# A fused decoder of two layers: expert weights spread by DMA, and new orders of work in three phases

## The reference

```python
x = ln(x + self_attention(x))            # layer 0: 16 heads, window of 32
x = ln(x + cross_attention(ctx, x))      # layer 0: one head of 128
x = ln(x + experts(x))                   # layer 0: 8 experts of 512, gelu, 2 of 8 by softmax
x = ln(x + state_space(x))               # layer 1: returns x + out itself, so x counts twice
x = ln(x + cross_attention1(x, ctx))     # layer 1: 16 heads of 64, inner width 1024
x = ln(x + experts1(x))                  # layer 1: 8 experts of 256 and a shared one, silu gate
```

```python
combined = sum_e w[:, e] * down_e(h_e(x))    # w from the top 2 of the router's logits
```

## Time and profile before

| | |
|---|---|
| median of 3 runs | 2001.07 us (1999.9 to 2002.27) |
| profiled execution | 1998.59 us, of which 1996.9 us are the span from first to last instruction |
| granted TensorE clock, mean | 0.941 of full |
| busy in the span | PE 88%, DVE 80%, ACT 59%, POOL 42% |
| moved by DMA | 264.97 MB, 133 GB/s in the mean |

### The profile page before, as it was taken

How to read it: one execution, slowest core, us unless ns; L and a number is a source line. 1 busy time by engine, 2 the same in 40 slices (tenths; PEclk the granted TensorE clock), 3 DMA queues, 4 the chain that set the end, 5 groups by cost and what they waited for, 6 DMA issues and landing times. The chain is left out here.

```text
span 1996.9 us, 34496 instructions
## 1 busy us (share of the span) xinstructions
PE 1750.6 (88%) x10381; PEld 1266.5 (63%) x10381; DVE 1593.3 (80%) x2986; ACT 1186.7 (59%) x1868; POOL 830.3 (42%) x705
## 2 busy tenths in 40 slices
PE   4886888699956379999999999999999999994997
PEld 3554656688842256666667666766666676654886
DVE  3884676678867379988998999899889988966887
ACT  2441332577732167777777777777777777754553
POOL 4660111223342373636364545455454546322333
PEclk9997998699976589999999999999999999997998
DMA  5101775100000079898989888989888998971000
GB/s 192 77 0 62 301 279 233 43 1 0 1 0 0 32 157 206 174 192 178 193 175 192 184 189 178 186 186 182 188 179 191 179 196 173 190 127 72 6 5 10
DMA packets 623534, 264.97 MB, mean 133 GB/s; under 512 B 601565, under 2 KB 605693, under 8 KB 622717
## 3 DMA queue, kind: packets, MB, share of 16 engines
q1 hardware_dynamic: 623468, 264.19, 57.1%
HBM read 112.24 MB, written 0.92 MB: 57 GB/s over the span
## 5 line engine op out<-in xcount | busy, mean ns | idle before, releaser
L2234 DVE SCALAR_TENSOR_TENSOR xa_h<-xa_psum,xa_rinv,xa_h 128x500 f16<-128x500 f32 x672 | 452.5, 729 | 0.7 <-ACT xa_h L2349 0.7
L2333 ACT ACTIVATE xa_psum<-xa_psum,xa_negmax 128x1500 f32<-128x1500 f32 x224 | 332.7, 1485 | 198.0 <-DVE xa_negmax L2219 198.0
L2349 ACT ACTIVATE xa_h<-xa_psum,xa_rinv 128x1000 f16<-128x1000 f32 x448 | 372.2, 883 | 82.5 <-DVE xa_rinv L2226 81.2
L2215 DVE TENSOR_REDUCE xa_psum<-xa_psum 128x1 f32<-128x1000 f32 x224 | 269.5, 1203 | 88.1 <-PE xa_psum L2089 88.1
L2087 PE MATMUL xa_psum<-xa_c_hi,xa_q_hi 128*128 128x500 f32 x672 | 282.9, 421 | 28.5 <-DVE xa_h L2234 18.3
L2112 PE MATMUL xa_psum<-xa_prT,xa_n_hi 128*128 128x512 f16 (+1 forms) x768 | 272.9, 355 | 2.4 <-DMA xa_prT<-xa_h 1.5
L2114 PE MATMUL xa_psum<-xa_prT,xa_n_lo 128*128 128x512 f16 (+1 forms) x768 | 270.7, 352 | 0.0
L2113 PE MATMUL xa_psum<-xa_prT,xa_n_hi 128*128 128x512 f16 (+1 forms) x768 | 270.7, 352 | 0.0
L2088 PE MATMUL xa_psum<-xa_c_lo,xa_q_hi 128*128 128x500 f32 x672 | 262.5, 391 | 0.0
L2089 PE MATMUL xa_psum<-xa_c_hi,xa_q_lo 128*128 128x500 f32 x672 | 262.2, 390 | 0.0
L2219 DVE TENSOR_REDUCE xa_negmax<-xa_psum 128x1 f32<-128x512 f32 x224 | 154.9, 691 | 25.8
(11 more groups left out here) (303 smaller groups left out, 3613.8 us busy)
## 6 DMA issues: line engine op xcount, KB each, us to landing
ctxN<-in_ctxP SPq DMA_DIRECT2D x16, 1536.0 KB, 9.2
xa_ctxP<-in_ctxP SPq DMA_DIRECT2D x32, 768.0 KB, 4.4
ctxT<-in_ctxT SPq DMA_DIRECT2D x16, 1500.0 KB, 6.3
xa_ctxT<-in_ctxT SPq DMA_DIRECT2D x32, 750.0 KB, 4.9
xa_prT<-xa_h SPq DMA_TRANSPOSE x192, 5.5
up<-in_F_up SPq DMA_DIRECT2D x1, 2048.0 KB, 9.2
down<-in_F_down SPq DMA_DIRECT2D x1, 2048.0 KB, 13.3
gate<-in_F_gate SPq DMA_DIRECT2D x1, 1024.0 KB, 4.8
```

The source lines that it names most:

```text
L2215: nc.vector.tensor_reduce(psum[:, bank + 1, W:W + 1], psum[:, bank:bank + 2, 0:W], AX.XY, ALU.max)\
L2234: nc.vector.scalar_tensor_tensor(h[:, H_SLOT[s], 1, a:z], psum[:, bank + j, 0:W], rinv[:, s % 2, :], h[:, H_SLOT[s], 0, a:z], ALU.mult, AL ...
L2333: nc.scalar.activation(psum[:, bank:bank + 3, 0:W], psum[:, bank:bank + 3, 0:W], ACT.Exp, bias=negmax[:, s % 2, :], accum_out=rs[:, s % 2, ...
L2349: nc.scalar.activation(h[:, H_SLOT[s], 0, a * W:z * W].rearrange("p (a c) -> p a c", c=W), psum[:, bank + a:bank + z, 0:W], ACT.Identity, ...
```

## The change

Six edits.

1. **Spread weights (expert phases).** The transposes, the copies from PSUM and POOL's copy are gone. At the end of routing the weights of all pairs are transposed once on PE, copied once (ACT in layer 0, DVE in layer 1), and stored by 16 DMAs of SP to an array in DRAM, rows by expert; the routing phase waits for the stores. In the expert phase SP loads, for each chunk, two halves of four experts, broadcast to 128 partitions, 1 MB each.
2. **PSUM waits.** The tail's transposes share no bank with spread products any more.
3. **State space.** `bout` is added by PE: a product of a row of ones with the bias row starts the accumulation in PSUM, and DVE adds twice the residual in the same operation as before. POOL's two additions are gone. PE multiplies `chosen` ahead of the tail's transposes.
4. **Self attention.** The bias row is added to all of `x_tok` once, on DVE, ahead of the steps. DVE, PE, ACT and POOL get another order; `attend` is cut in two.
5. **First cross attention.** The logits move to a step of their own (lag 6). The values are cut in three, tops in two halves, and all engines' orders change.
6. The scratch area that the compiler keeps for dynamic DMAs is set to 2,048 bytes.

```diff
# experts: load of the spread weights, and their use
+            def load(i, half):
+                sp.wait_ge(part_ready, last(i, (half + 1) * EH, NE))
+                sp.sem_inc(issuing, 1)
+                sp.dma_start(spread[:, half * EH:(half + 1) * EH, :].rearrange("p e (g t) -> p e g t", g=CK),
+                             k.weight_rows[layer][half * EH:(half + 1) * EH, bass.ds(i * CK, CK), :].partition_broadcast(128))\
+                    .then_inc(spread_loaded[half], 16)
-                def spread_weights(e):
-                    for p in range(CK):
-                        done = nc.tensor.transpose(psum[:, 6 + e % 2, p * 128:(p + 1) * 128],
-                                                   wc[:, p, e:e + 1].to_broadcast([128, 128]), k.ident[:, :])
-                    done.then_inc(spread_ready, 1)
-                def keep_spread(e):
-                    nc.vector.tensor_copy(spread[:, e % 3, :].rearrange("p (b s) -> p b s", b=CB),
-                                          psum[:, 6 + e % 2, :].rearrange("p (b s) -> p b s", b=CB)[:, :, 0:S])\
-                        .then_inc(spread_kept, 1)
+                    dve.wait_ge(spread_loaded[e // EH], (i + 1) * 16)
+                    weights = split(spread[:, e, :])[:, :, 0:S]
...
# routing
+            sp.wait_ge(turned_kept, 1)
+            for g in range(PAIRS):
+                sp.dma_start(k.weight_rows[layer][:, g, :], weights_T[g * E:(g + 1) * E, :]).then_inc(rows_stored, 16)
+            sp.wait_ge(rows_stored, PAIRS * 16)
+            def turn_weights():
+                pe.wait_ge(weights_ready, 1)
+                nc.tensor.transpose(psum[:, 7, 0:128], k.expert_weights[:, :, :].rearrange("p g e -> p (g e)"), k.ident[:, :])\
+                    .then_inc(turned_ready, 1)
+            if layer == 1:
+                turn_weights()
             for g in range(FOLDS):
+                if g == FOLDS - 1:
+                    turn_weights()
+                    pe.wait_ge(turned_kept, 1)
...
# state space, POOL, PE and DVE
-                pool.tensor_tensor(xb[:, :, :], x, k.bout_row1[:, :].unsqueeze(1).to_broadcast([128, CK, D]), ALU.add)
-                pool.tensor_tensor(xb2[:, :, :], xb[:, :, :], x, ALU.add).then_inc(xb2_ready, 1)
+            def bias(i):
+                pe.wait_ge(r_ready, last(i))
+                nc.tensor.matmul(psum[:, 6, :], ones[:, :], k.bout_row1[0:1, :].unsqueeze(1).to_broadcast([1, CK, D]),
+                                 start=True, stop=False)
-                if previous is not None:
-                    tail(previous, alone=False)
                 pe.wait_ge(step_done, this(i, CHOSEN, NV))
                 nc.tensor.matmul(psum[:, 5, 0:CT], k.wso1[:, :], chosen[:, :], start=True, stop=True)\
                     .then_inc(state_out_ready, 1)
+                if previous is not None:
+                    tail(previous, alone=False)
+                bias(i)
+                nc.vector.scalar_tensor_tensor(r[:, :, :], k.x_tok[:, bass.ds(i * CK, CK), :], 2.0,
+                                               psum[:, 6, :].rearrange("p (c d) -> p c d", c=CK), ALU.mult, ALU.add)\
```

More of the change, by code:

```diff
@@ L490, in _, with attend @@
             pe.wait_ge(qs_zeroed, 1)
+            def attend(j, p, part):
+                if part == 0:
+                    pe.wait_ge(prT_kept, this(j, p + 1, PER))
+                    pe.wait_ge(v_kept, this(j, p + 1, PER))
+                    pe.wait_ge(o_kept, this(j, p, PER))
+                for hp in range(part * HP // 2, (part + 1) * HP // 2):
+                    for half in range(2):
+                        done = nc.tensor.matmul(psum[half * SP:(half + 1) * SP, 6, hp * 16:(hp + 1) * 16],
+                                                prT[:, p, hp, half * SP:(half + 1) * SP],
+                                                vexp[:, p, half, hp * 16:(hp + 1) * 16], start=True, stop=True)
+                if part:
+                    done.then_inc(o_ready, 1)
             def step(i, s):
@@ L536, in step @@
                     done.then_inc(v_ready, 1)
+                at = pair(i, s, "output")
+                if at:
+                    j, p = at
+                    pe.wait_ge(o_kept, this(j, p + 1, PER))
+                    pe.wait_ge(t.r_ready, this(j, p, PER))
+                    nc.tensor.transpose(psum[:, 7, 0:128], on[:, p, :], k.ident[:, :]).then_inc(oT_ready, 1)
+                at = pair(i, s, "attend")
+                if at:
+                    attend(*at, 0)
                 at = pair(i, s, "norm")
@@ L670, in step @@
                                          psum[0:2 * S, 4:6, :], ACT.Copy).then_inc(prT_kept, 1)
+                at = pair(i, s, "output")
+                if at:
+                    j, p = at
+                    act.wait_ge(oT_ready, this(j, p + 1, PER))
+                    act.wait_ge(y_ready, last(j, p + 1, PER))
+                    nc.scalar.activation(oT[:, p, :], psum[:, 7, 0:128], ACT.Identity, bias=k.bv0[:, :])\
+                        .then_inc(oT_kept, 1)
                 at = pair(i, s, "norm")
@@ L694, in context_attention_phase @@
     Q4 = C // 4
-    steps = PairSteps(project=0, scores=1, transpose=2, values=3, output=4, norm=5)
+    steps = PairSteps(project=0, scores=1, transpose=2, values=3, output=4, norm=5, logits=6)
     PER, pair, n = steps.PER, steps.pair, steps.count
@@ L786, in values @@
             def values(p, part):
[L788 removed]
+                for kt in range(part * KT // 3, (part + 1) * KT // 3):
                     for half in range(2):
@@ L818, in step @@
                     done.then_inc(scores_ready, 1)
+                at = pair(i, s, "logits")
+                if at:
+                    pe.wait_ge(qp_kept, n(i, s, 0))
+                    pe.wait_ge(t.r_ready, n(i, s, 5))
+                    pe.wait_ge(t.feat_stored, n(i, s, 6))
+                    t.tensor_logits(pe, *at, psum[:, 7, 384:384 + E])
+                at = pair(i, s, "transpose")
+                if at:
+                    j, p = at
+                    pe.wait_ge(exp_ready, this(j, p + 1, PER))
+                    pe.wait_ge(even_kept, this(j, 2 * p, 2 * PER))
+                    transposes(j, p, 0)
+                    pe.wait_ge(odd_kept, this(j, p, PER))
+                    transposes(j, p, 1)
                 at = pair(i, s, "output")
@@ L849, in step @@
                     values(p, 0)
+                at = pair(i, s, "norm")
+                if at:
+                    pe.wait_ge(t.logits_kept, n(i, s, 6))
+                    pe.wait_ge(oT_kept, n(i, s, 4))
+                    t.tensor_transpose(pe, *at, psum[:, 7, 256:384])
+                at = pair(i, s, "values")
+                if at:
+                    values(at[1], 1)
                 at = pair(i, s, "project")
```

304 lines of the change are left out of this document (122 added, 182 removed).

## The result

The changed kernel takes 1935.1 us in the median (1934.5 to 1936.0 over 4 runs) against 2001.7 us; the ratio is 0.9662, 95% interval 0.9649 to 0.9675. Predicted were 1944 us, 1922 to 1962. The profiled execution's span is 1933.5 us, 63.4 less than before.

| stage | before | after | measured | forecast |
|---|---|---|---|---|
| setup and self attention | 168.1 | 153.1 | -15.0 | -4 |
| first cross attention | 192.5 | 178.8 | -13.7 | -18 |
| routing 0, to PE's first product | 21.8 | 24.9 | +3.1 | +7 |
| expert phase 0 | 208.7 | 198.6 | -10.1 | -15 |
| state space | 88.2 | 74.7 | -13.5 | -12 |

A forecast was written before the change was run, and what follows sets the result against it. No common limit: TensorE 88% and VectorE 80% busy over seven barrier-closed phases, each bound differently. Terms -4 - 18 + 7 - 15 - 12 + 2 - 16.5 = -56.5 us gave 1942 or 1944.6, stated as 1944 us, range 1922 to 1962.

The forecast's parts named there:

- I take 7.25 us per pair: 15 x 0.24 = -4 us: Self attention: POOL's kexp holds DVE's norm 1.1 us, so a pair goes from 7.49 to 7.25 us; bounds -17 and +5.
- self attention gains its idle time: Rival: POOL's products miss the norm; 6.3 to 6.5 us per pair, mask additions 97 us apart, 1932 us; chance 0.17.
- 11 pairs x 1.5 = -16.5 us, and -18 with the incomplete steps: First cross attention: PE no longer waits for scaled query and logits copy, 1.5 us per pair; bounds -20 and -8.
- The context loads did not hold the stage: Rival, first cross attention: context loads land 1 to 2 us later, gain 8 instead of 18, 1954 us; chance 0.14.
- +7 and +2: Routing phases 0 and 1: weight stores, 16 x 0.44 + 2.6 = 9.6 us after the copy, lengthen them by 7 and 2 us.
- -15 became -10.1, and -16.5 became -12.6: Expert phases 0 and 1: removing spread transposes and copies saves 15 and 16.5 us; bounds -11.5 and -19 each.
- the term for waits, 3 us: Expert phase 1: PE's own waits at the spread transposes go too, about 3 us.
- the 0.36 forecast for the transposes: Expert phases: each removed group of four PE transposes saves 0.36 us, 32 groups giving 11.5 us per phase.
- I took 7 us for 2 MB: Expert phases: the new weight loads, 2 MB per chunk, need 7 us at the context loads' rate and stay hidden.
- -12 forecast: State space: chosen multiplied at once, POOL's additions gone; 3 x 3.8 = -11.4 us, -12 with first chunk's taps; bounds -6 and -17.
- self attention and state space at their best: Low end of the whole kernel's range: 1944 - 22 = 1922 us.
- The loads would have held a chunk: Rival "slower", experts: one DMA engine serves the broadcast loads, 2250 us; decides from below 1.5 engines on; chance 0.03.

The follow-up runs named there:

- Experiment 7: Changed kernel with the weights laid out by expert and pair, so one 64 KB store replaces the 16 of 4 KB in routing: 1933.4 us, ratio 0.9664.
- experiment 4: Changed kernel with ACT storing x_feat of the tail one hidden block earlier in expert phase 0: 1929.4 us, ratio 0.9643.
- experiments 5 and 6: Changed kernel, both expert phases: four transposes per expert back on PE (1952.6 us); or one 448-column copy per expert back on DVE (1948.9 us).
- experiment 5: Changed kernel with four transposes of a constant column per expert back on PE in both expert phases, no DVE copies: 1952.6 us.
- kernel 8: Changed kernel with the tail's transposes ahead of the product of chosen again in the state space phase, bias product kept on PE: 1943.5 us.

## Why the prediction was right or wrong

**The sum** was right within its range, and partly for the wrong reasons: self attention gave 11 us more than forecast, routing 6 us more, and the first cross attention and the experts 13 us less. That these misses cancel to 7 us is luck.

**Self attention: the step that failed is "I take 7.25 us per pair: 15 x 0.24 = -4 us".** The mechanism was forecast and is there: the norm is held by POOL's first product, at a mean of 1.00 us. Two sizes were wrong. The hold is 0.7 us and not 1.1; and the mean of 7.49 us per pair from the earlier trace rows, against which the new step was set, mixes two kinds of steps. The first five steps fill the pipeline, and only the last of them has a norm. The 6th and the last mask addition of the kernel before:

```profile
62.36 1.09 DVE L583 TENSOR_TENSOR sa_sm<-sa_psum,window_mask 128x896 f32<-128x896 f32 x1 [1.24 <-PE sa_psum L510]
...
141.22 1.08 DVE L583 TENSOR_TENSOR sa_sm<-sa_psum,window_mask 128x896 f32<-128x896 f32 x1
```

The ten full steps from 62.36 to 141.22 took 7.89 us each. In the changed kernel they run from 60.34 to 129.72, 6.94 each:

```profile
L593 DVE TENSOR_TENSOR sa_sm<-sa_psum,window_mask x16: 1027/1078/1092, 29.3 to 129.7; 128x896 f32<-128x896 f32 x16
```

The full step lost 0.95 us, not 0.24: 9.5 us. For the other 5.5 us the forecast had no term: the filling lost 2.0 (33.5 to 31.1, less a start 0.5 later), the drain 3.5, of which up to 2.3 us can be scatter (the drain takes 21.8 to 24.1 us with the changed kernel's code). The first and last mask additions start 100.4 us apart, neither the 109 of the forecast nor the rival's 97. The rival "self attention gains its idle time" had the size (16 us in this stage) but not the cause: it needed the norm to be missed by POOL.

The Trainium skill, SBUF — State Buffer ("SBUF: two separate sides"), says that DVE's operations in a two-port mode or with two SBUF operands exclude a GpSimd operation that reads SBUF, for the whole instruction of the one that comes first. The traces of the kernel before and of three orders after it agree on which operations are held: only the norm (1.15 us in the timeline) and the subtraction (up to 2.42 us), never the mask addition from PSUM (1.03 to 1.09 us) or the maximum.

**First cross attention: the term "11 pairs x 1.5 = -16.5 us, and -18 with the incomplete steps" was too large.** The forecast step of 9.2 to 9.5 us is right: 9.38 (the maxima from 208.15 to 301.91 in the timeline). But the full step before was 10.73 us (220.53 to 327.82), not 10.9, and there are ten: -13.5 us. The incomplete steps gave nothing: filling +2.6 us, drain -2.8, both no more than what these two parts scatter by with the same code (below). The context loads did not hold the stage: no maximum or score waits for them in the changed kernel, PE waits once, 0.9 us, for the values' context, and the load of `ctxT` lands in 6.2 us. In two of the later profiles PE waited once, 2.6 us, for a load of `ctxT`, so there is little room.

**Routing: +7 and +2 were too much.** The three parts of the sum are each smaller: the weights' copy came 15.8 us into the phase, not 16.8; an issue took 0.34 us and not 0.44 (5.39 us for 16, above); and from the last issue to the next phase 1.9 us passed instead of 2.6. Experiment 7 shows that the issues were what counted in layer 0. In layer 1 the last issue ended at 1773.1 and DVE's low parts at 1774.0, and the next phase began at 1775.1: 1.9 us behind the one, as in layer 0, and 1.0 us behind the other, as in the kernel before. The two end together, at no cost.

**Experts: -15 became -10.1, and -16.5 became -12.6.** The first weighings of a chunk, as in the earlier trace rows:

```profile
L1475 DVE SCALAR_TENSOR_TENSOR moe_acc<-moe_psum,down_bias,moe_spread x4: 676/684/685, 367.4 to 502.0; 128x448 f32<-128x448 f32 x4
...
L1478 DVE TENSOR_TENSOR moe_acc<-moe_psum,moe_spread x4: 618/624/625, 1785.3 to 1891.4; 128x448 f32<-128x448 f32 x4
```

A chunk takes 44.9 and 35.4 us (forecast 43.5 and 34.5). In phase 0 the forecast missed that PE, once earlier, waits for ACT's store of x_feat (experiment 4: 6.4 us). With that store moved a chunk takes 43.5 us, as forecast. In phase 1 the term for waits, 3 us, was too large: in the kernel before, PE's waits at the transposes come to 0.7 us in that phase, and 2.9 us only if its weight loads are read in their place. And the phase is not the sum of its parts (experiments 5 and 6). The steps without a tail took 3.64 us instead of 4.08, which is more than the 0.36 forecast for the transposes; experiment 5 shows that the transposes alone cost these 0.44 us, and that DVE's copies cost nothing there.

**The loads of the weights** were hidden, but not for the reason given. I took 7 us for 2 MB from the context loads' rate; the rows of the changed kernel say, for all loads and then for the first and the second load of phase 0:

```profile
ctxT<-in_ctxT SPq DMA_DIRECT2D x16, 1500.0 KB, 6.2
...
moe_spread<-weight_rows SPq DMA_DIRECT2D x16, 1024.0 KB, 8.6
...
moe_spread<-weight_rows SPq DMA_DIRECT2D x1, 1024.0 KB, 9.2
...
moe_spread<-weight_rows SPq DMA_DIRECT2D x1, 1024.0 KB, 14.4
```

One load of 1 MB takes 8.6 us in the median. Of the first two, asked for at once at 355.2, the first landed at 364.3 and the second at 370.1, so 2 MB took 14.9 us, twice the forecast. The first weighing needs only the first half and starts at 367.4, 3.1 us later; the fifth, which needs the second half, starts at 386.2. In phase 1 the room was 1.4 us (landed at 1783.9, first weighing at 1785.3). No other load had less than 8 us.

**State space: -12 forecast, -13.5 measured.** DVE's addition of the output product, once per chunk, gives the period, before and after:

```profile
L1740 DVE TENSOR_TENSOR ss_r<-ss_psum,ss_xb x4: 683/692/692, 609.3 to 667.4; 128x512 f32<-128x512 f32 x4
...
L1750 DVE SCALAR_TENSOR_TENSOR ss_r<-x_tok,ss_psum x4: 686/687/689, 571.8 to 618.6; 128x512 f32<-128x512 f32 x4
```

That is 15.6 us instead of 19.4 in the mean of three (15.3 to 16.1 singly), the forecast 3.8 us less. The bias product delayed the outputs by 0.8 to 1.1 us, not 0.5, and the product of chosen was 0.85 us faster in one of the three chunks that carry a tail, and 0.65 in another, where the granted clock was higher; in the third it took 1.86 us as before.

**Sums of the prediction that do not come out.** The low end of the range takes 22 us off for "self attention and state space at their best"; the bounds named for them are 13 and 5 us, 18 together, which gives 1926. The loads would have held a chunk of 43.5 or 34.5 us from below 1.8 and 2.3 engines on, not 1.5. The second cross attention is 1127.5 us long, not 1,110. None of the three changes the forecast.

## What to carry to other kernels

Take the period of a pipeline from its full steps alone: the mean from the first start to the last mixes in the filling, and here it hid 0.4 us per step (7.49 against 7.89). When work is taken from an engine, ask what it then arrives at earlier: a wait that was always covered (here ACT's store into a shared PSUM bank) becomes the new limit, and moving that one instruction gave 6.4 us. Two edits that shorten the same chain don't add: 10.1 and 7.6 us gave 13.5. To learn what each of two removed works was worth, put them back one at a time and read the steps singly: here PE's work counted in the steps without norms, DVE's in those with them.

## What the runs showed of the hardware

- While POOL multiplied two SBUF operands, DVE's normalisation (SBUF to SBUF) and subtraction (two SBUF operands) stood still until a POOL instruction ended; the mask addition from PSUM and the maximum over one SBUF operand ran at their own pace (1.08 us). In the timelines the norm ended 0.11 us behind the first of POOL's two products, the subtraction 0.93 us behind the second.
- The same code of the first cross attention took 175.9 to 182.2 us. The full steps were equal (9.35 to 9.40 us). The filling took 52.4 to 55.1 us, and the drain 28.4 us at a granted clock of 0.90 to 33.6 us at 0.71. The drain window of the changed kernel and of kernel 8:

```profile
300.00:331.00 31.00, 20.32 (x201) 15.88 (x197) 13.60 (x34) 6.57 (x21) 5.64 (x16) 0.87 0.29 111
```

```profile
300.00:334.00 34.00, 23.59 (x198) 18.80 (x197) 13.17 (x34) 6.57 (x21) 5.64 (x16) 0.72 0.26 96
```

- The drain of self attention followed the granted clock as well: with the changed kernel's code 24.1 us at 0.57, 23.4 at 0.62 and 21.8 at 0.72.
- A broadcast load of 1 MB to 128 partitions, in runs of 2 KB, landed in 8.6 us; the 1.5 MB loads of `ctxT` in 6.2 us.
- Sixteen stores of 4 KB cost SP 0.34 us each, one store of 64 KB the same 0.34 us once.
